# ScalarE's own tile of gathered rows goes to GpSimd in the last full pass of each sum

## What is computed

```python
# sums 1 and 2: relational layers, 8 edge types
xt  = jnp.einsum('nd,rde->rne', x, W)
agg = segment_sum(xt[rel, src], dst)
x   = relu(agg + x @ SW + b)
# after the second: x1 = layernorm(x0 + x)
# sum 3: plain
feat = relu(x1 @ W1 + b1); h = feat * d_invsqrt
agg  = segment_sum(h[src], dst)
out  = layernorm(x1 + (feat - agg * d_invsqrt) @ W2 + b2)
```

## Time and profile before

| | |
|---|---|
| median of 3 runs | 9507.16 us (9503.04 to 9524.47) |
| profiled execution | 9512.93 us, span 9511.2 us |
| GpSimd busy | 4561.2 us (48%), 4822 instructions |
| TensorE matmul busy | 3350.8 us (35%) |
| VectorE busy | 1975.7 us (21%) |
| ScalarE busy | 130.3 us (1%), 430 instructions |
| single rows by SyncE | 3712 for each sum |
| single rows by ScalarE | 3584 for each sum |
| gathers by GpSimd (L808) | 1604, 1590 and 1583 |
| mean busy share of the 16 DMA engines | one tenth in every slice |

### The profile page before, as it was taken

How to read it: one execution, slowest core, us unless ns; L and a number is a source line. 1 busy time by engine, 2 the same in 40 slices (tenths; PEclk the granted TensorE clock), 3 DMA queues, 4 the chain that set the end, 5 groups by cost and what they waited for, 6 DMA issues and landing times.

```text
span 9511.2 us, 99977 instructions
## 1 busy us (share of the span) xinstructions
PE 3350.8 (35%) x13625; PEld 2381.6 (25%) x13626; DVE 1975.7 (21%) x3147; ACT 130.3 (1%) x430; POOL 4561.2 (48%) x4822
## 2 busy tenths in 40 slices
PE   3333433434333434344343343344222222222223
PEld 2222222222222322222222222224222222222223
DVE  4322332323232212122121221122001001001001
ACT  0000000000000000000000000000000000000000
POOL 4545444444444444444544444444554454455454
PEclk6666666666666666666666666665555555555555
DMA  1111111111111111111111111111111111111111
GB/s 49 40 40 42 36 38 40 41 39 39 38 43 41 36 40 44 40 40 42 40 47 40 40 41 40 46 42 35 40 42 39 40 42 40 37 43 41 37 43 39
DMA packets 239445, 385.74 MB, mean 41 GB/s; under 512 B 106473, under 2 KB 137532, under 8 KB 239100
## 3 DMA queue, kind: packets, MB, share of 16 engines
q0 software_dynamic: 153984, 315.67, 12.7%
q1 hardware_dynamic: 61768, 60.65, 2.1%
q10 hardware_dynamic: 23348, 6.44, 0.3%
HBM read 356.60 MB, written 25.75 MB: 40 GB/s over the span
## 4 chain that ended last, share of the span: by engine, by line
SPq 49%; issue 37%; ACTq 8%; PE 3%; DMA 1%; DVE 1%; another core or an unknown queue 0%; ACT 0%; DVEq 0%
SPq L867 38%; ACTq L867 7%; SPq L863 6%; ACTq L863 1%; PE bank L1008 1%; SPq L684 1%; SPq L686 1%; SPq L846 1%; SPq L683 1%; PE bank L980 0%; SPq L109 0%; SPq L850 0%; SPq L856 0%; PE bank L1565 0%
## 5 line engine op out<-in xcount | busy, mean ns | idle before, releaser
L808 POOL DMA_INDIRECT rows<-x_d,idx x1590 | 1504.0, 946 | 1687.7 <-ACT idx L771 1202.7
L808 POOL DMA_INDIRECT rows<-in_x_dram,idx x1604 | 1518.1, 946 | 1651.4 <-ACT idx L771 1186.7
L808 POOL DMA_INDIRECT rows<-h_d,idx x1583 | 1504.7, 951 | 1505.4 <-ACT idx L771 1026.0
L1008 PE MATMUL bank<-r_S,rows 128*128 128x128 f32 x6644 | 1115.6, 331 | 2023.5 <-DMA rows<-in_x_dram 998.4
L1008 PEld LDWEIGHTS bank<-r_S,rows 128*128 128x128 f32 x6644 | 1058.0, 242 | 2083.9 <-issue 2062.0
L1211 PE MATMUL bank<-r_S,rows 128*128 128x64 f32 x3322 | 745.3, 411 | 2093.9 <-DMA rows<-h_d 1479.7
L1211 PEld LDWEIGHTS bank<-r_S,rows 128*128 128x128 f32 x3322 | 733.6, 328 | 2108.1 <-issue 2107.4
L1104 DVE COPY r_agg<-bank 128x512 f32<-128x512 f32 x476 | 320.5, 687 | 2969.1 <-PE bank L1008 2059.7
L1255 DVE TENSOR_TENSOR acc<-acc,bank 128x64 f32 x238 | 52.7, 222 | 2093.2 <-issue 962.4
L1046 DVE TENSOR_TENSOR r_S<-bank,key 128x1792 f32<-128x1792 f32 x238 | 479.0, 2013 | 0.7 <-issue 0.7
L980 PE MATMUL bank<-r_agg,w1s 128*128 128x512 f32 (+1 forms) x512 | 448.5, 1044 | 42.5 <-DVE r_agg L1104 24.1
(11 more groups left out here) (157 smaller groups left out, 1357.9 us busy)
## 6 DMA issues: line engine op xcount, KB each, us to landing
rows<-in_x_dram SPq DMA_DIRECT2D x3712, 0.5 KB
rows<-x_d SPq DMA_DIRECT2D x3712, 0.5 KB
rows<-h_d SPq DMA_DIRECT2D x3712, 0.5 KB
rows<-in_x_dram ACTq DMA_DIRECT2D x3584, 0.5 KB
rows<-x_d ACTq DMA_DIRECT2D x3584, 0.5 KB
rows<-h_d ACTq DMA_DIRECT2D x3584, 0.5 KB
rows<-in_x_dram,idx POOLq DMA_INDIRECT x1604
rows<-x_d,idx POOLq DMA_INDIRECT x1590
```

What stands on the lines that cost most here:

```text
L808: pool.indirect_dma_start(out=self.c.rows[:, self.place(s), :], out_offset=None, in_=self.table[:, :], in_offset=bass.IndirectOffsetOnAxis ...
L1008: mm = pe.matmul(agg_ps[j][:, bass.ds(offs[j * KG + k], TK)], c.rows[:, g.place(h * KG + k), :], S[:, pb, j * KG + k, :], start=False, sto ...
```

## The change

GpSimd gathers tile 55 in pass 28 too (the last full pass), 54 + 1 = 55 gathers there, as in pass 0. `ends_of(i)` is 1 for i = 28 and 0 before: (i + 4) >> 5. ScalarE issues rows only for passes 1 to 27: its two blocks of rows in a pass are skipped for i = 28, and the block at the end of pass 27, which began the rows of pass 28, is skipped too. For i = 28 it waits for its list and raises the semaphores of its rows by what the 128 DMAs would have raised them, so that TensorE's wait on them stays as it is; TensorE waits for one gather more in that pass.

```diff
+ENDING_BITS = (IT - 1).bit_length()
+ENDING = 1 << ENDING_BITS
...
+def ends_of(i):
+
+    return (i + (ENDING - (IT - 1))) >> ENDING_BITS
...
-                        if s < skip or (part is FULL and s in (OWN[:BY_ACT] if first else OWN)):
+                        if s < skip or (part is FULL and s in others):
...
-            iteration(q, 0, FULL, skip, first=True)
-            with pool.Fori(1, IT) as i:
-                iteration(q, i, FULL)
+            iteration(q, 0, FULL, skip, OWN[:BY_ACT])
+            with pool.Fori(1, IT - 1) as i:
+                iteration(q, i, FULL, others=OWN)
+            iteration(q, IT - 1, FULL, others=OWN[:BY_ACT])
...
-                pe.wait_ge(self.landed[h], i * (gathered * 16) + (gathered + 1) * 16)
+                pe.wait_ge(self.landed[h], i * (gathered * 16) + ends_of(i) * 16 + (gathered + 1) * 16)
...
+    ends = ends_of(i)
     at_once = AT_ONCE[g.turns]
     own = range(at_once, LISTS)
-    with act.If(i > 0):
+    with act.If(i > ends * IT):
         g.load_own(nc, act, BY_ACT, own[:-4])
+    act.end_ifs()
+    with act.If(i > IT - 2):
+        g.list_there(act, BY_ACT, q, i)
+        for share in g.own[BY_ACT]:
+            act.sem_inc(share, P // OWN_SEMS * 16)
     act.end_ifs()
     for p in range(PR):
         g.take(act, p, q, i + 1)
         if p < PR // 2:
-            with act.If(i > 0):
+            with act.If(i > ends * IT):
                 g.load_own(nc, act, BY_ACT, own[-4:][2 * p:2 * p + 2])
...
-    with act.If(i < IT - 1):
+    with act.If(i < IT - 2):
         g.own_free(act, BY_ACT, q, i + 1)
         g.load_own(nc, act, BY_ACT, range(at_once))
```

More of the change, by code:

```diff
@@ L795, in run, with iteration @@
     def run(self, pool, ready, stored):
-        def iteration(q, i, part, skip=0, first=False):
+        def iteration(q, i, part, skip=0, others=()):
             for p in part.pairs:
```

## The result

The kernel changed takes 9549.18 us (median of 7 runs, 9541.03 to 9561.78), the kernel before in the same comparison 9520.27 (9503.04 to 9524.78): a ratio of 1.0036, 95% interval 1.0024 to 1.0047, that is, 34 us slower (23 to 45). The profiled execution took 9558.43 us, its span is 9556.8, against 9512.93 and 9511.2.

A forecast was written before the change was run, and what follows sets the result against it. The prediction took SyncE's queue of row DMAs, 49% of the chain of waits, as the bound. Gathers' price 23 plus tests 2 gave +25 us: 9538 on the profiled execution, 9532 in the median's terms, range 9494 to 9554.

The forecast's parts named there:

- parts 1 and 3: ScalarE's row DMAs leave the last full passes: -14.5 us, second sum; leftover gathers move beside SyncE's rows: 7, 17, 8 more.
- my sum: Predicted cost of gathers beside SyncE's rows in each sum's last full pass, at 1.21 us each: +8.5, +6.1, +9.7, together 24.3.
- third 8 x 1.21 = 9.7: Last full pass of the third sum: 8 more gathers beside SyncE's rows at 1.21 us each cost 9.7 us.
- the deep rate: Cost to SyncE's rows of each gather deep in a back-to-back run: 1.06 us, on top of 50.3 for 128 rows.
- the rival of the long run: Merged gather runs cost SyncE's rows the deep rate from their start in the last full passes: 37.3 us, 9546 to 9552; chance 0.15.
- part 4: Added tests and register work on ScalarE and TensorE in each of the 87 full passes: +2 us, 0 to 6.
- The rows don't pay for the moved gathers: Rival: gathers cost SyncE's rows nothing, and ScalarE's 14.5 us lateness in the second sum's last pass goes: 9495; chance 0.15.
- this trace's two rates: SyncE issues a row every 0.39 us while GpSimd is idle, every 2.6 us deep in a run of gathers.

The follow-up runs named there:

- the tests alone: The kernel changed with its new bit set in no pass, so no row or gather moves: ratio to the kernel before 1.0000 on kind B, 1.0004 on kind A.
- most of them held: The kernel changed, with ScalarE waiting for SyncE's 128 rows before the second pair's leftover indices, holding 23 of 37 gathers: 1.0016 to the kernel before, kind A.
- the second sum alone: The change made in the second sum only, the other sums as in the kernel before: ratios 1.0006 and 1.0010 on two chips of kind A.

## Why the prediction was right in its mechanism and off in its size

*The base.* I set +25 us on 9507.16, a median of 3 runs. Seven runs gave 9520.27. Of the 17 us between 9532 and 9549, 13 are this base, and the rest is that the step measured 29 us between the medians (34 by the ratio) and not 25; the three runs ranged over 21 us, and I took their middle without asking what it was worth.

*Who ends the passes, and what comes forward (parts 1 and 3): right.* The tile of ScalarE in the second sum was late by its own rows, and its wait went (on kind B it is the gain). I counted 42, 53 and 46 gathers beside SyncE's rows; two executions had 49, 57, 48 and 43, 56, 46. In the first sum the number depends on where in the burst SyncE's pass starts. I expected stretches of 90, 106 and 91 us: they took 97, 105, 104 and 88, 105, 102.

*The price of the gathers: near in the first sum, too high in the second, too low in the third.* From SyncE's first row of the last full pass to the first row of the next sum (or to the end of the span) took, over the profiles of kind A in which the leftover gathers of that sum weren't held, in us:

| | code as before | changed | difference | my sum |
|---|---|---|---|---|
| first sum | 176.8, 183.0, 177.4, 176.5, 177.4 | 189.2, 179.7 | +6 | +8.5 |
| second | 194.9, 200.2, 203.9 | 200.8, 200.1, 201.2, 200.2 | +1 (+6 to the first of them) | +6.1 |
| third | 116.3, 116.1, 114.1, 117.7 | 137.7, 136.5, 134.7 (48, 46, 45 gathers), 146.2 (57) | +20, and +30 | +9.7 |

The second sum's stretch came out as forecast (105 us for 106); what was off is its base, since the one trace that I had read shows 85.6 us where two others with this sum as before have 91.2 and 88.2. The failed step is "third 8 x 1.21 = 9.7", against 20 measured. The 8 gathers were nearly right (10 and 8 more), the price wasn't: with 46 to 48 gathers the stretch is 102 to 103 us, which is the deep rate from its start (50.3 + 1.06 x 46 = 99), the number of the rival of the long run. I priced the added gathers and left the 38 old ones at what they had cost. In the trace before, these 38 stand in four bursts with pauses between them, (81.3 - 50.3)/38 = 0.82 us each; in all four profiles with the third sum changed and nothing held, the 45 to 57 stand in two, (103.6 - 50.3)/48 = 1.11 each. The merging of bursts made the old ones dearer, and SyncE's timeline shows how. The first line is one of two bursts of 14 gathers before (17.5 us); the others are the burst of 37 after, in its first 14 gathers, the next 14 and the last 9:

```profile
9452.31 16.54 SPq L867 DMA_DIRECT2D rows<-h_d  x22
...
9437.86 16.93 SPq L876 DMA_DIRECT2D rows<-h_d  x21
9456.21 16.80 SPq L876 DMA_DIRECT2D rows<-h_d  x7
9472.30 11.20 SPq L876 DMA_DIRECT2D rows<-h_d  x5
```

In the first 14 gathers of a burst SyncE gets 21 or 22 rows through, half of them in its first 5 us, in the next 14 only 7. At 0.393 us a row the first 14 cost it (17.5 - 21 x 0.393)/14 = 0.66 us each, the next 1.05. Each burst has its cheap start once, and the merged one has given two away. Counted so, the gathers cost 26 us of the stretch before and 45 after, 19 of the 22 us that it grew by. In the first two sums the number of bursts stayed the same (four and three) and the price nearly so (0.90 to 0.96 us a gather, and 0.98 to 0.96). The number of bursts alone isn't the measure, though: in the second sum 37 gathers took 88.2 us in three bursts (19, 14 and 4, the tests alone) and 87.4 in two (23 and 14, most of them held).

That the whole came near my 25 is in part luck: by the table the third sum was 10 us too cheap in my sum and the first two together some 8 too dear. And the forecast holds only for the kind of chip whose trace it was read from; on the other kind its sign is wrong (two chips, -15 and -16 us), five of the eight chips of the later runs are of that kind, and nothing in one trace could say that.

*The tests (part 4): +2 expected, 1.0004 (0.9994 to 1.0013) measured.* The profiles of before and after also drift apart in the ordinary passes: up to SyncE's first row of the last full pass by +7, -9 and +8 us in the three sums. This is scatter: up to that row the first sum took 3082 to 3097 us in nine profiles of kind A, and 3082.0 and 3091.4 with one and the same kernel (the second sum alone) on two chips.

*The rivals.* "The rows don't pay for the moved gathers" was set at -12 us, and that is what kind B gives (-15, -16). I weighed it at 0.15 by this trace's two rates, which speak against it and against the page DMA: Bandwidth & Descriptors of the Trainium skill (section SWDGE vs HWDGE vs iDMA), which says that an engine of the DMA takes the two sorts of queues in turn. On kind B nothing contradicts the page; on kind A the rows of SyncE go 6 to 7 times slower deep in a run of gathers, and instructions that issue no DMA are slow there too (below).

## What to carry to other kernels

Where a gather makes the neighbours' queues slow, a transfer that is brought forward isn't free because it is early: count how many gathers fall on the engine that ends the pass, and price the whole stretch, the gathers that were there already too, since a burst's first gathers are cheap and its later ones dear, and merging short bursts gives the cheap starts away. A tile handed from a late queue to an idle engine gains its wait only if the work that this queue held back doesn't land on the next to finish. Gains and losses of 0.3% can have opposite signs on two chips, so look first at which regime the profile is from.

## What the runs showed of the hardware

Eight chips fell into two kinds by one thing. While gathers run, SyncE's register moves (11,481 in each profile) take 0.24 us in the mean on kind A, 30% of them over 0.5 us, and 0.029 on kind B; outside of gathers 0.05 and 0.03. ScalarE's take 0.18 against 0.029. The profiles of one kind (9 and 11) agree within 0.015 us. The same moves of one line, in the third sum of the kernel before (A) and of the tests alone (B), shortest, median and longest in ns:

```profile
L867 SPq MOVE rows<-h_d x3712: 2/29/1397, 6496.5 to 9475.9; - x196
...
L876 SPq MOVE rows<-h_d x3712: 29/29/38, 4079.8 to 6001.2; - x196
```

A register move issues no DMA, so on kind A the instruction streams themselves are slow beside GpSimd's gathers, and not only the transfers. Each row is such a move and a DMA instruction, and both are slower there: the DMA instruction takes SyncE 0.33 us beside gathers and 0.23 otherwise. VectorE's branches take 0.39 against 0.09 us (kernel before). TensorE's register arithmetic isn't slowed: 0.033 us on either kind, beside gathers or not. The granted clock, 0.60 on A and 0.65 on B, is far from such a factor. A gather itself takes the same on both, 0.95 us and 0.30 to the next. The kernel is bound by SyncE on A and by GpSimd on B, where the chain that ended last, in the profile of the kernel changed, reads:

```profile
POOL 61%; issue 23%; PE 8%; ACTq 4%; DVE 2%; DMA 1%; POOLq 0%; DVEq 0%; ACT 0%; SPq 0%
```

Hence 9520 and 6077 us for one program. What sets the kind of a chip, no run shows; the streams' fetching of instructions is a candidate that wasn't tried.
